# Expert row tiles of 256 rows with one load of weights per pair, in a fused Mamba and mixture-of-experts layer

## Time and profile before

| | |
|---|---|
| median of 3 runs | 5622.27 us |
| profiled execution | 5651.79 us |
| its span | 5650.1 us |
| mean granted PE clock | 0.874 of full |
| DVE busy | 4604.8 us, 82% |
| PE busy | 4426.2 us, 78% |
| POOL busy | 3587.6 us, 63% |
| ACT busy | 3183.0 us, 56% |
| DMA | 563.53 MB in 357156 packets, 100 GB/s on average |
| pairs | 160 |

### The profile page before, as it was taken

One profiled execution on the slowest core, in us unless ns is written; L12 is line 12 of the kernel. 1 busy time (PEld: TensorE's weight loads), 2 busy tenths in 40 slices (PEclk: granted clock), 3 DMA queues, 4 the chain that ended last, 5 costly groups with the idle time before them and its releaser, 6 DMA issues.

```text
span 5650.1 us, 75862 instructions
## 1 busy us (share of the span) xinstructions
PE 4426.2 (78%) x20928; PEld 3080.2 (55%) x20928; DVE 4604.8 (82%) x7212; ACT 3183.0 (56%) x5088; POOL 3587.6 (63%) x2252
## 2 busy tenths in 40 slices
PE   3777888788788888877887887788888878887773
PEld 1455555555555555555555555555555555655652
DVE  4888888888888888888888888888978888878730
ACT  3555555565556556656665665665566565655521
POOL 3566666655566557776655777766576775777732
PEclk6788888899898888998999898899989889998985
DMA  4122222233333324333221433322144332554544
GB/s 118 53 79 77 77 79 79 68 118 112 123 102 105 104 64 112 110 106 92 73 76 60 113 112 106 92 70 79 58 131 127 100 98 90 152 147 122 156 130 121
DMA packets 357156, 563.53 MB, mean 100 GB/s; under 512 B 40433, under 2 KB 203378, under 8 KB 356610
## 3 DMA queue, kind: packets, MB, share of 16 engines
q1 hardware_dynamic: 245906, 390.43, 22.7%
q0 software_dynamic: 49152, 67.27, 5.9%
q10 hardware_dynamic: 61680, 100.97, 5.4%
HBM read 440.66 MB, written 186.05 MB: 111 GB/s over the span
## 4 chain that ended last, share of the span: by engine, by line
PE 33%; DVE 16%; issue 11%; ACT 10%; POOL 7%; DMA 6%; SPq 5%; ACTq 1%; DVEq 0%; POOLq 0%
PE ps L801 8%; DVE hs L1024 6%; DVE acc L1040 4%; DMA xin<-X_slots 3%; PE ps L948 3%; POOL fx L521 3%; PE ps L880 2%; POOL dBx L471 2%; PE ps L846 2%; DVE xc L1009 2%; PE ps L766 2%; DMA Y_slots<-xin 2%; PE ps L790 2%; ACT ps L625 2%; PE ps L816 2%
## 5 line engine op out<-in xcount | busy, mean ns | idle before, releaser
L471 POOL TENSOR_TENSOR dBx<-dtx,Bbc 128x1024 f32<-128x1024 f32 x1024 | 2442.3, 2414 | 1050.2 <-DVE hs L1024 1043.1
L1024 DVE TENSOR_TENSOR_SCAN hs<-ps,dBx 128x512 f32<-128x512 f32 x2048 | 2402.6, 1205 | 178.4 <-ACT ps L625 169.2
L801 PE MATMUL ps<-ident,hs 128*128 128x128 f32 x8192 | 1409.6, 313 | 566.5 <-DVE acc L1040 475.8
L625 ACT ACTIVATE ps<-dt,A 128x512 f32<-128x512 f32 x2048 | 1390.7, 688 | 774.1 <-DVE hs L1024 744.2
L801 PEld LDWEIGHTS ps<-ident,hs 128*128 128x128 f32 x8192 | 1068.2, 159 | 1044.4 <-DVE acc L1040 780.9
L1040 DVE SCALAR_TENSOR_TENSOR acc<-ps,C_tok,acc 128x512 f32<-128x512 f32 x1792 | 1280.8, 736 | 211.8 <-PE ps L801 194.1
L503 POOL DMA_INDIRECT X_slots<-xs,slots x256 | 256.5, 1002 | 429.2 <-DVE slots L1158 343.8
L521 POOL DMA_INDIRECT fx<-Y_slots,slots x256 | 403.8, 1577 | 137.9 <-DMA fx<-shared 60.7
L1009 DVE SCALAR_TENSOR_TENSOR xc<-ps,conv_w,xc 128x511 f32<-128x511 f32 (+2 forms) x384 | 284.7, 741 | 136.0 <-ACT xc L585 131.2
L948 PE MATMUL ps<-xsT,wx 128*128 128x128 f32 x2560 | 356.4, 296 | 27.2 <-ACT xsT L706 27.2
L948 PEld LDWEIGHTS ps<-xsT,wx 128*128 128x128 f32 x2560 | 338.5, 211 | 45.1 <-issue 41.0
(11 more groups left out here) (166 smaller groups left out, 6191.9 us busy)
## 6 DMA issues: line engine op xcount, KB each, us to landing
Bbc<-B_scratch SPq DMA_DIRECT2D x512, 256.0 KB
wx<-in_experts SPq DMA_DIRECT2D x320, 384.0 KB
Y_slots<-zeros ACTq DMA_DIRECT2D x228, 256.0 KB
xin<-X_slots SPq DMA_DIRECT2D x320, 128.5 KB
Y_slots<-xin SPq DMA_DIRECT2D x320, 128.0 KB
xt<-in_x SPq DMA_DIRECT2D x32, 512.0 KB, 4.0
shared<-xt ACTq DMA_DIRECT2D x32, 512.0 KB, 2.6
fx<-shared SPq DMA_DIRECT2D x32, 512.0 KB
```

Of the source, the lines that this page charges most:

```text
L471: pool.tensor_tensor(dBx[u % 3][:], dtx[b % 2][:, 2 * h:2 * h + 2, :], Bbc[g % NBB][:, n % CH:n % CH + 1, :].broadcast_to([P, 2, T]), ALU. ...
L625: act.activation(psA[s % 2][:], dt[b % 2][:, j, :], ACT.Exp, scale=A[:, j, n:n + 1]).then_inc(s_dA, 1)
L801: i = pe.transpose(psH[w % 2][:, j * P:(j + 1) * P], hs[(n * CT + j) % NHB][:, t * P:(t + 1) * P], ident[:])
L1024: dve.tensor_tensor_scan(hs[s % NHB][:], psA[s % 2][:], dBx[s // 2 % 3][:, s % 2, :], 0.0, ALU.mult, ALU.add).then_inc(s_scan, 1)
```

## The change

A pair is now one tile of 256 rows of one expert (`PAIR = 2 * P`). Rows of an expert are rounded up to 256 instead of 128, so the fixed numbers of pairs per group become 31, 31, 31, 31, 23, 15, 11, 11. `wx` holds one set of weights; a pair has one load of weights, one of 256 rows and one store, each with its value loads halved. The transposes write the two halves of the rows side by side, and the gate and up projections are 4 matmuls of 256 columns instead of 8 of 128. The blocks of zeros behind the experts' rows have 256 rows. `ROWS` grows, so there are 2 x 121 clears instead of 2 x 114. The tables on DVE get shorter. The table `AT` has new numbers throughout; among them the first of `ACT_clear`, which was -102.16 and is 32.21.

```diff
 AT = {
-    "ACT_clear": [-102.16, -16.39, -15.63, -15.06, -13.69, 3.98, 5.55, 19.77, 37.85, 38.27, 38.27, 38.27, 38.27,
-        38.27, 38.27, 38.27, 41.43, 43.01, 82.8, 93.78],
+    "ACT_clear": [32.21, 32.37, 32.37, 32.37, 41.74, 41.82, 41.82, 41.82, 41.82, 41.82, 41.82, 43.39, 43.39, 43.39,
+        43.39, 43.39, 48.35, 63.54, 71.56, 74.36, 74.36, 135.92],
...
-    "SP_experts": [109.22, 123.94, 128.62, 130.16, 138.72, 140.58, 143.48, 145.84, 152.76, 164.44, 164.93, 172.31],
-    "SP_finish": [138.47, 155.2, 171.45],
+    "SP_experts": [112.34, 120.12, 128.73, 129.83, 139.66, 142.26, 146.62, 150.94, 158.61, 164.99, 169, 174.24],
+    "SP_finish": [139.48, 158.59, 169.99],
...
-    tiles = [(2 * n * T + NE * (P - 1)) // P for n in groups]
-    tiles = [n + n % 2 for n in tiles]
+    PAIR = 2 * P
+    tiles = [(2 * n * T + NE * (PAIR - 1)) // PAIR for n in groups]
...
-    ROOM = CAP + P
-    ROWS = NE * ROOM + 28 * P
+    ROOM = CAP + PAIR
+    ROWS = NE * ROOM + 34 * P
...
-    OFF = [groups[g - 2] * T + P if g >= NG - 2 else 0 for g in range(NG)]
+    OFF = [groups[g - 2] * T + PAIR if g >= NG - 2 else 0 for g in range(NG)]
...
-    pairs_to = [sum(tiles[:g + 1]) // 2 for g in range(NG)]
+    pairs_to = [sum(tiles[:g + 1]) for g in range(NG)]
...
-        wx = [sb(f"wx{i}", [P, 2, WIDE]) for i in range(2)]
+        wx = [sb(f"wx{i}", [P, WIDE]) for i in range(2)]
...
                             for e in range(NE):
-                                r = sp.value_load(ends[g % 2][0:1, e:e + 1], min_val=0, max_val=ROWS - P)
-                                sp.dma_start(X_slots[g % 2][bass.ds(r, P), :], zeros[:, 0:ROW]).then_inc(s_padded[g % 2], 16)
+                                r = sp.value_load(ends[g % 2][0:1, e:e + 1], min_val=0, max_val=ROWS - PAIR)
+                                sp.dma_start(X_slots[g % 2][bass.ds(r, PAIR), :], zeros.rearrange(
+                                    "p (a d) -> (p a) d", a=2)).then_inc(s_padded[g % 2], 16)
...
-                        for i in range(2):
-                            e = sp.value_load(where[g % 2][0:1, 1, tile + i:tile + i + 1], min_val=0, max_val=NE * P)
-                            r = sp.value_load(where[g % 2][0:1, 0, tile + i:tile + i + 1], min_val=0, max_val=ROWS - P)
-                            sp.dma_start(wx[k][:, i, :], a["experts"].rearrange("e p f -> (e p) f")[
-                                bass.ds(e, P), :]).then_inc(s_wx[k], 16)
-                            sp.dma_start(xin[k][:, i, :], X_slots[g % 2][bass.ds(r, P), :]).then_inc(s_xin[k], 16)
+                        e = sp.value_load(where[g % 2][0:1, 1, tile:tile + 1], min_val=0, max_val=NE * P)
+                        r = sp.value_load(where[g % 2][0:1, 0, tile:tile + 1], min_val=0, max_val=ROWS - PAIR)
+                        sp.dma_start(wx[k][:], a["experts"].rearrange("e p f -> (e p) f")[bass.ds(e, P), :]).then_inc(s_wx[k], 16)
+                        sp.dma_start(xin[k][:], X_slots[g % 2][bass.ds(r, PAIR), :].rearrange("(i p) d -> p i d", p=P)).then_inc(
+                            s_xin[k], 16)
...
-                        for i in range(2):
-                            r = sp.value_load(where[g % 2][0:1, 0, tile + i:tile + i + 1], min_val=0, max_val=ROWS - P)
-                            sp.dma_start(Y_slots[g % 2][bass.ds(r, P), :], xin[k][:, i, 0:D]).then_inc(
-                                s_Y_out[k], 16)
+                        r = sp.value_load(where[g % 2][0:1, 0, tile:tile + 1], min_val=0, max_val=ROWS - PAIR)
+                        sp.dma_start(Y_slots[g % 2][bass.ds(r, PAIR), :].rearrange("(i p) d -> p i d", p=P),
+                                     xin[k][:, :, 0:D]).then_inc(s_Y_out[k], 16)
...
-                                i = pe.transpose(psE[:, (m * KD + k) * P:(m * KD + k + 1) * P],
+                                i = pe.transpose(psE[:, (2 * k + m) * P:(2 * k + m + 1) * P],
                                                  xin[p % 2][:, m, k * P:(k + 1) * P], ident[:])
...
-                            for o in range(2):
-                                for k in range(KD):
-                                    i = pe.matmul(psE[:, o * HALF + m * P:o * HALF + (m + 1) * P],
-                                                  w[:, m, (2 * k + o) * P:(2 * k + o + 1) * P],
-                                                  xsT[:, (m * KD + k) * P:(m * KD + k + 1) * P], start=(k == 0),
-                                                  stop=(k == KD - 1))
+                            for k in range(KD):
+                                i = pe.matmul(psE[:, o * HALF:(o + 1) * HALF], w[:, (2 * k + o) * P:(2 * k + o + 1) * P],
+                                              xsT[:, k * PAIR:(k + 1) * PAIR], start=(k == 0), stop=(k == KD - 1))
```

More of the change, by code:

```diff
@@ L28 @@
[L28 to L33, removed]
@@ L88 @@
+    "SP_finish": [139.48, 158.59, 169.99],
+    "SP_inputs": [-64.21],
+    "SP_results": [126.29, 129.57, 135.81, 141.99, 143.17, 148.52, 152.17, 163.86, 167.45, 169.8, 175.63, 179.15],
 }
@@ L164, in build @@
         ended, finished = ended + take, finished + len(fins_in[b])
-    group_of_pair = [g for g in range(NG) for _ in range(tiles[g] // 2)]
+    group_of_pair = [g for g in range(NG) for _ in range(tiles[g])]
     ctx = ExitStack()
@@ L228, in build @@
         taken, table = 0, []
-        for n in (NE * (CAP // P), NT, NE, NE, NE, NT * NE, NT, NT):
+        for n in (NE * (CAP // PAIR), NT, NE, NE, NE, NT * NE, NT, NT):
             table.append(few[M0:M0 + 1, taken:taken + n])
@@ L232, in build @@
         full, tile_no, fills, cum0, cum1, beyond, at_row, at_expert = table
-        over = beyond[:, 0:NE * (CAP // P)].rearrange("p (e n) -> p e n", e=NE)
+        over = beyond[:, 0:NE * (CAP // PAIR)].rearrange("p (e n) -> p e n", e=NE)
         full, beyond = full.rearrange("p (e n) -> p e n", e=NE), beyond.rearrange("p (i e) -> p i e", e=NE)
@@ L326, in stores @@
         def stores(p, k):
-            return 32 * ((p - k) // 2 + 1)
+            return 16 * ((p - k) // 2 + 1)
         block = ctx.enter_context(nc.Block())
@@ L367, in experts @@
                         g, k = group_of_pair[p], p % 2
-                        tile = 2 * (p - pairs_to[g]) + tiles[g]
+                        tile = p - pairs_to[g] + tiles[g]
                         yield b
@@ L960, in results @@
                             i = pe.matmul(psE[:, m * D:(m + 1) * D], ge[:, m * P:(m + 1) * P],
-                                          wx[p % 2][:, m, KD * 2 * P:WIDE], start=True, stop=True)
+                                          wx[p % 2][:, KD * 2 * P:WIDE], start=True, stop=True)
                         i.then_inc(s_down_e, 1)
@@ L970, in _ @@
             dve.memset(where[1], 0).then_inc(s_consts, 1)
-            for k in range(CAP // P):
-                dve.memset(full[:, :, k:k + 1], float(k * P)).then_inc(s_consts, 1)
+            for k in range(CAP // PAIR):
+                dve.memset(full[:, :, k:k + 1], float(k * PAIR)).then_inc(s_consts, 1)
             for k in range(NT):
@@ L1191, in group_tiles @@
                 dve.wait_ge(s_meta, done + 2)
-                dve.tensor_tensor(over, cum0.rearrange("p (e o) -> p e o", o=1).broadcast_to([1, NE, CAP // P]),
+                dve.tensor_tensor(over, cum0.rearrange("p (e o) -> p e o", o=1).broadcast_to([1, NE, CAP // PAIR]),
                                   full, ALU.is_gt).then_inc(s_meta, 1)
@@ L1205, in group_tiles @@
                     [1, NT, NE]), ALU.is_le).then_inc(s_meta, 1)
-                dve.tensor_scalar(fills, fills, -float(P), float(ROOM), ALU.mult, ALU.add).then_inc(s_meta, 1)
+                dve.tensor_scalar(fills, fills, -float(PAIR), float(ROOM), ALU.mult, ALU.add).then_inc(s_meta, 1)
                 dve.wait_ge(s_meta, done + 12)
@@ L1217, in group_tiles @@
                 dve.wait_ge(s_meta, done + 17)
-                dve.scalar_tensor_tensor(out=w[:, 0, :], in0=tile_no, scalar=float(P), in1=at_row, op0=ALU.mult,
+                dve.scalar_tensor_tensor(out=w[:, 0, :], in0=tile_no, scalar=float(PAIR), in1=at_row, op0=ALU.mult,
                                          op1=ALU.add).then_inc(s_meta, 1)
```

92 lines of the change are left out of this document (48 added, 44 removed), and 30 rows, old and new, of the table AT.

## The result

The changed kernel takes 5772.1 us (median of 4 runs, 5765.6 to 5786.1) against 5631.7 us of the kernel before in the same comparison: ratio 1.024, 95% interval 1.0211 to 1.0268. It is slower, as forecast, but by 140 us and not by 63; the time lies above the range of 5625 to 5760.

What follows compares the result with a forecast made beforehand. No engine was taken as full: pairs cost 2.3 us during scans by work and waiting, and pair latency rules the end. Terms summed to +63 us on the 5622.3 us median, giving 5685 us, range 5625 to 5760.

Steps and rivals of the forecast that it cites:

- The period lists: Pairs and finishes per period: 12, 11, 12, 12, 12 pairs in periods 27 to 31, one in 32; last finish in 33.
- 24 and 8: Last group: +24 us for 11 end-stage pairs instead of 8, +8 us for two finishes in order in period 31.
- A lone finish: Batch 31's finish behind batch 30's, after the very last pair: a chain that cannot overlap, +33 us.
- the post stage: Last batch's post stage, period 30: four more pairs and two fewer finishes about cancel, +5 us, bounds -15 and +30.
- +12 and -6: Zero stores moved into batch 0: +12 us for blocking ACT during scans, -6 us for the earlier start.
- 2 x 8.53 x 34/28 = 21 us: Upper bound of the stall on ACT's queue from the moved zero stores and the clears behind them in batch 0.
- A cheaper pair: Fewer SP loads and stores bring rows sooner: half of PE's `xin` wait saved up to period 28, -53 us, bounds 0 and -107.
- steady stage: Up to period 28, 147 pairs instead of 132: 15 more at 2.3 us each, +35 us.
- (a): Rival: PE's row wait of 0.73 us per pair goes wholly off the path, -107 not -53; 5631 us, chance 0.19.
- (b): Rival: TensorE's weight loads set the pace; halving them saves 1.06 us per pair, 156 us; 5529 us, chance 0.05.
- (c): Rival: another wait covers the cheaper pair's saving in every period, 0 instead of -53; 5738 us, chance 0.20.
- (d): Rival: the last two finishes overlap with pairs because the last result leaves early, -33; 5652 us, chance 0.06.

Runs made afterwards that it cites:

- experiment 6: Kernel before, with SP's reads ahead of its waits and rows issued before weights: 5556.9 us, 0.9827; with the reads alone: 5574.4 us, 0.9901.

## Why the prediction was wrong

**Right in direction and in most parts of the end.** The period lists held: 184 pairs, 13 of them behind the last scatter (two left over and the last group's 11), two finishes alone. The last group's first pair started 31.3 us after the last scatter's issue, where it was 25.4: +6, said 5. From its first `xsT` to its last result the group took 111.1 us instead of 83.4, +28, where 24 and 8 were said. A lone finish took 32 us, said 33. Together the end took 64 us more, said 70; the post stage 1, said 5. In the table by stages, form and count alone give 72 behind the last scatter, and the order takes some 8 back.

**Failed: what has no price in the sum.** The prediction worked out the change's new order table only where a strand moved far (the clears, the finishes), and took the rest as free. It cost 70 us at this form and count (5755 against 5685) and is nearly the whole miss: the change cost 77 us more than was said (140 for 63), of which 70 are the order, 11 the zero stores (17 for 6), and -4 form and count (53 for 57). In it, SP's loads of B moved up to 8 ticks later, and POOL, which had never waited for them, waited 212 us. The step that failed is the list of the parts: it has no line for the B loads, although ten of their 16 places moved later, and none for the other strands. That SP's tables are about half of the 70 was shown by exchanging them in both directions; the other half is unexplained.

**Failed: the size of the stall at the zero stores.** +12 and -6 were said. Batch 0 became 32 us longer, and moving them, with the other clears, cost the whole kernel 17 (medians) to 30 us (spans). The bound of 2 x 8.53 x 34/28 = 21 us was wrong: it gave 10.4 us to the second store and as much to the clears behind it, by scaling the old row with the size of the stores, and the store took 16.39 us and the three clears 22.82.

**Mis-sized, and cancelling.** A cheaper pair: -53 said, half of the wait. With form alone, the stretch from batch 3 to the last scan went from 4844 to 4739 us: -105, nearly all of the upper bound of 107; the whole kernel gained 88 us. In the other three comparisons of old with new form, the new one took 94, 119 and 105 us off this stretch. More pairs: +35 said for the steady stage, measured 4739 to 4794, +55. That is 3.7 us for each of 15 pairs and not 2.3; in the other three comparisons of 160 with 184 pairs the same stretch grew by 43, 25 and 11 us, 2.9 to 0.7 us each, so a pair has no one price there, and why is not shown. In sum form and count gave 53 us (5632 to 5685), where I had said 57 (63 without the 6 of the moved stores). That 5685 is also the predicted number is partly luck: two terms were off in opposite ways, and the kernel before had a median of 5622 us when the forecast was made and of 5632 here.

**The rivals.** (a) was right on its own mechanism: the wait goes off the path in full. With the form alone it fell from 149.5 to 35.3 us, and experiment 6 has the same gain from sooner rows alone, with two loads of weights. (b) is refuted: the same kernel with short matmuls is no slower. The Trainium skill, page "TensorE: Matmul & The Clock Gate", section "Back-to-back issue gap", says that the weight load and the matmul set the spacing together, and the estimate from its figures was 0.5 us per pair for the short ones; this case's traces do not agree, with 0.06 us at most (1.95 against 1.89). (c) is refuted by the same -105. (d) did not happen by itself, since the order put the finishes behind; where they were moved it gave 18 to 26 us. No rival held the order of other work.

## What to carry to other kernels

Where a change comes with a new fixed order, price the order on its own, for work that the change does not touch as well: here the form of the pairs was worth -88 us, their greater number +141, the order that came with them +70, and the moved zero stores +17. A load that comes late can be made earlier by reading its address ahead of the wait and by issuing first what is needed first; that gave all of the form's gain without its padding. Look at what stands behind a large store in its queue: ahead of the first batch the two zero stores were 17 us cheaper than in the middle of batch 0. Another queue for them was not tried.

## What the runs showed of the hardware

Issuing a DMA on ACT's queue is not always short: 0.73 us for the first store of zeros in the changed kernel, 16.39 for the second, and up to 21.4 us for a clear of 256 KB behind them, where the median of the clears is 0.62 us. These are the instructions of both lines, ns min/median/max:

```profile
L551 ACTq DMA_DIRECT2D X_slots<-xin x2: 732/8560/16389, 145.1 to 145.9; - x2
...
L559 ACTq DMA_DIRECT2D Y_slots<-zeros x242: 497/618/21408, 162.4 to 2031.4; - x121
```

Matmuls of 256 columns are hardly cheaper per column in this type than those of 128: 0.267 us busy each against 2 x 0.139 = 0.278, and nothing of it in the time.

Reading one number for a DMA's address on SP takes about 0.44 us here: medians of 0.27 us for the read and 0.15 and 0.02 for the two instructions behind it, at the value loads of the kernel before.
